# Two residual layers on two images: a convolution that splits each row once, keeps it in a ring and joins its sums, with the attention's instructions in another order

## The chip, the cores and the metric

The kernel runs on one core of a Trainium2 chip. The metric is the device time of one execution in microseconds. Five engines take part: PE multiplies matrices, DVE, ACT and POOL work on tensors, and SP issues all DMAs from one queue. Each runs its own list of instructions in order and waits on semaphores. PE writes only to PSUM (8 banks of 512 f32 per partition), and POOL doesn't read PSUM.

## The reference

The input x holds two images of 128 channels x 128 x 128 pixels. Two layers follow one another, each with a group normalisation `_gn` over 4 channels and all pixels of an image, and each added to its input:

```python
x = x + _L0_conv_ref(_gn(x), ...)   # windowed attention
x = x + _L1_conv_ref(_gn(x), ...)   # 3x3 convolution, 128 to 128 channels, bias
```

The attention works on g = clip((x * ac_w + ac_b) * x, 0, 6), takes q, k and v from it by a 384 x 128 matrix, does softmax(q k' / sqrt(8)) v in 16 heads of 8 channels within windows of 8 x 8 pixels, and multiplies by a 128 x 128 matrix.

## The kernel before

The channels are the partitions, and one image (`img`, 64 KB per partition) is resident. For each image the stages are: coefficients of the first normalisation, 32 units of attention, coefficients of the second normalisation, 16 strips of convolution. While image 0 is convolved, strips of image 1 are loaded into the rows that come free, and DVE takes their statistics (L784).

A unit of attention is 8 windows, 512 pixels. It passes through a software pipeline that spans about eight iterations; `iterations` calls `one(i, m, live)` on every engine, and the written order inside `one` is the order of that engine's list. The order isn't planned by any program: it is written out by hand, with iteration n working on unit n + lead. The steps of a unit are:

- DVE makes the affine part (L700), the product with x (L658) and the clip (L672). ACT casts it to half precision, `g_hi` (L503), and POOL takes the rest, `g_lo` (L369).
- PE projects q and k (`project`, L824 to L826, three half-precision products in place of a full-precision one) and v (`v_rows`, L842). ACT and DVE split q and k into two halves (L493 and L690, L478 and L688), and ACT copies v (L487).
- SP writes the halves of k and q to DRAM (L247, L248) and reads them back in another layout, `k_pl` (L266) and `q_bd` (L258).
- PE computes `scores` in four parts (L855), and DVE takes each part's row maxima (L646). Part p + 1 writes over part p in PSUM, so it waits for its maxima. PE transposes the maxima (L938), ACT and DVE split them (`m_pair`, L497 and L693), and SP copies them by four small DMAs as two further rows of `q_bd` (L274).
- PE computes the transposed scores with the maxima taken off (`scores_t`, L867), ACT exponentiates (L451), and PE multiplies with v and sums (`weigh`, L886, and L894 in parts 1 and 3). ACT and DVE divide (L458, L460, L639), POOL corrects the quotient by one Newton step (`quotient`, L361 and L363), PE projects it (L953), ACT scales (L470), POOL adds it to the image (L376), and DVE takes the statistics for the next normalisation (L684).

A strip of the convolution is 8 output rows. ACT normalises ten input rows into `cx` (L522). Each pair of neighbouring output columns comes from four planes of differences and sums of columns (64 columns each) instead of six products per row: DVE makes the planes 0 and 2 (L740), POOL the planes 1 and 3 (L399). ACT casts each to half precision (L528), and DVE takes the rest (`low`, L744). PE does 9 matmuls per plane, 36 of 512 columns per strip (L824 to L826), into one bank per plane; two sets of four banks alternate. ACT starts the odd columns from plane 1 with the bias (L512), DVE adds the planes by four instructions of 512 elements (`outputs_of`, L724), POOL adds the input (`residual`, L387), and SP stores the strip (L295). All ten rows of a strip are made anew, so two of ten are made twice.

What sets the order in a strip: DVE's list alternates L740 and L744 of strip t + 1 with the L724 of strip t - 1. POOL's L387 may start when all four L724 of its strip are done; `cx` may be overwritten when both DVE and POOL have made their planes.

## Time and profile before

| | us |
|---|---|
| median of 3 runs (1294.46 to 1301.38) | 1300.46 |
| profiled execution | 1303.66 |
| its span | 1301.9 |
| PE busy | 1058.8 (81%) |
| DVE busy | 1024.6 (79%) |
| ACT busy | 793.4 (61%) |
| POOL busy | 605.2 (46%) |
| mean granted clock of PE | 0.946 of 2.4 GHz |

The stages, read from the first and last instructions of their lines: the attention's residual L376 runs from 117.0 to 491.7 us and from 743.8 to 1118.1, the convolution's first normalisation starts at 498.97 in image 0, and the last instruction of the kernel ends at 1301.9. The time ahead of a stage's first L376 is the load, the coefficients and the filling of the pipeline.

An engine's busy time contains the time in which an instruction has started and stands still. A matmul's end is modelled: matmuls of 512 columns are 0.38 us long on the page and follow each other at 0.22.

### The profile page before, as it was taken

How to read it: one execution, taken by the hardware profiler on the slowest of the kernel's cores; microseconds unless marked ns; L12 is line 12 of the kernel's file. 1: busy time of each engine (PE TensorE's matmuls, PEld its weight loads, DVE VectorE, ACT ScalarE, POOL GpSimd, SP SyncE). 2: the span in 40 equal slices, each digit the busy share in tenths (PEclk: the TensorE clock that was granted, in tenths of full speed). 3: DMA queues.
4: the chain of work that ended last, by engine and by line, in shares of the span. 5: the costliest groups of instructions: out<-in, count | busy, mean ns of one | idle time of the engine just before them, and what ended most of it. 6: DMA issues, size and time to landing. Idle time of an engine off the chain costs nothing. (4 is left out here: it accounts for less than half of the span.)

```text
span 1301.9 us, 52825 instructions
## 1 busy us (share of the span) xinstructions
PE 1058.8 (81%) x23011; PEld 582.1 (45%) x23011; DVE 1024.6 (79%) x1315; ACT 793.4 (61%) x1295; POOL 605.2 (46%) x501
## 2 busy tenths in 40 slices
PE   1179999989998975887855999999999998498886
PEld 1045555555555542333322555555555555243332
DVE  6866787778887646999996677777787774599998
ACT  1147877777787764544412777777777776454442
POOL 7004444444444354555541344445445444366665
PEclk9999999999999996999885999999999999698998
DMA  7054444435444400222234544445444441001112
GB/s 284 25 147 122 134 130 132 140 113 145 123 133 127 138 19 1 97 98 97 97 114 139 138 130 137 127 128 140 133 132 129 138 141 30 1 33 48 49 50 80
DMA packets 114918, 140.60 MB, mean 108 GB/s; under 512 B 25088, under 2 KB 91008, under 8 KB 113664
## 3 DMA queue, kind: packets, MB, share of 16 engines
q1 hardware_dynamic: 114688, 137.23, 35.2%
q8 instruction: 182, 2.98, 1.0%
q14 instruction: 48, 0.39, 0.1%
HBM read 67.96 MB, written 67.11 MB: 104 GB/s over the span
## 5 line engine op out<-in xcount | busy, mean ns | idle before, releaser
L646 DVE TENSOR_REDUCE m_all<-ps 128x16 f32<-128x1024 f32 x256 | 312.8, 1222 | 134.2 <-PE ps L855 133.7
L369 POOL TENSOR_TENSOR g_lo<-work,g_hi 128x512 f16<-128x512 f32 x64 | 91.6, 1431 | 301.1 <-ACT g_hi L503 301.1
L361 POOL TENSOR_SCALAR work<-work 128x256 f32<-128x256 f32 x128 | 114.2, 892 | 210.2 <-DVE work L639 191.9
L824 PE MATMUL ps<-work,c_hi 128*128 128x512 f16 x384 | 153.5, 400 | 64.3 <-DVE work L744 64.3
L528 ACT CAST work<-work 128x640 f16<-128x640 f32 x128 | 91.9, 718 | 151.6 <-DVE work L740 118.0
L867 PE MATMUL ps<-q_bd,k_pl 128*64 128x256 f16 x2048 | 164.3, 283 | 18.2 <-DMA q_bd<-m_pair 13.0
L451 ACT ACTIVATE work<-ps,ws 128x1024 f32<-128x1024 f32 x128 | 142.7, 1115 | 40.8 <-PE ps L867 39.0
L855 PEld LDWEIGHTS ps<-k_pl,q_bd 48*64 48x64 f16 x8192 | 88.7, 111 | 155.1 <-issue 75.4
L744 DVE TENSOR_TENSOR work<-work 128x640 f16<-128x640 f32 x128 | 152.3, 1193 | 4.3 <-ACT work L528 4.2
L451 ACT ACTIVATE late_probs<-ps,ws 128x1024 f32<-128x1024 f32 x128 | 141.6, 1106 | 20.4 <-PE ps L867 20.4
L825 PE MATMUL ps<-work,c_lo 128*128 128x512 f16 x384 | 152.7, 398 | 0.0
L826 PE MATMUL ps<-work,c_hi 128*128 128x512 f16 x384 | 152.7, 398 | 0.0
L855 PE MATMUL ps<-k_pl,q_bd 48*64 48x64 f16 x8192 | 117.5, 198 | 39.5 <-DMA q_bd<-stack_scratch 27.5
L399 POOL TENSOR_TENSOR work<-work 128x640 f32<-128x640 f32 x64 | 113.5, 1774 | 51.0 <-DVE work L744 23.8
L387 POOL TENSOR_TENSOR work<-work,img 128x1024 f32<-128x1024 f32 x30 | 87.0, 2900 | 99.6 <-DVE work L724 99.6
L867 PEld LDWEIGHTS ps<-q_bd,k_pl 128*64 128x64 f16 x2048 | 93.5, 110 | 64.7 <-ACT late_probs L451 25.5
L639 DVE TENSOR_TENSOR work<-ps,work 128x512 f32<-128x512 f32 x128 | 87.3, 682 | 27.3 <-ACT work L460 27.3
L824 PEld LDWEIGHTS ps<-work,c_hi 128*128 128x128 f16 x384 | 38.8, 101 | 137.4 <-DVE work L744 96.4
L487 ACT COPY v_ext<-ps 64x256 f32<-64x256 f32 x256 | 93.1, 364 | 9.4 <-PE ps L842 4.8
L363 POOL TENSOR_TENSOR work<-work 128x256 f32<-128x256 f32 x128 | 93.2, 728 | 10.7
L740 DVE TENSOR_TENSOR work<-work 128x640 f32<-128x640 f32 x64 | 94.7, 1482 | 4.0 <-issue 2.4
L458 ACT ACTIVATE work<-ps 128x256 f32<-128x256 f32 x128 | 49.2, 384 | 74.8 <-PE ps L894 74.8
(128 smaller groups left out, 2008.7 us busy)
## 6 DMA issues: line engine op xcount, KB each, us to landing
stack_scratch<-work SPq DMA_DIRECT2D x128, 256.0 KB, 2.0
k_pl<-stack_scratch SPq DMA_DIRECT2D x128, 192.0 KB, 3.7
q_bd<-stack_scratch SPq DMA_DIRECT2D x256, 96.0 KB
stack_scratch<-work SPq DMA_DIRECT2D x128, 128.0 KB, 2.1
out_dram<-work SPq DMA_DIRECT2D x32, 512.0 KB, 2.6
img<-in_x_dram SPq DMA_DIRECT2D x8, 1024.0 KB, 13.5
img<-in_x_dram SPq DMA_DIRECT2D x16, 512.0 KB, 4.2
q_bd<-m_pair SPq DMA_DIRECT2D x256, 8.0 KB
```

The source lines that it names most:

```text
L361: g.tensor_scalar(near[h], near[h], -2.0, None, ALU.add).then_inc(less_done, 1)
L363: g.tensor_tensor(o_n[:, HALF * h:HALF * h + HALF], near[h], scaled[h], ALU.mult).then_inc(o_done, 1)
L399: g.tensor_tensor(plane[2 * k + 1], column(cx, 1), column(cx, c), op).then_inc(odd_planes, 1)
L451: a.activation(probs[h][:, p % 2, :], ps[:, ST_B:ST_B + 2, :].rearrange("p w t -> p (w t)"), ACT.Exp, scale=ws[:, R_EXP:R_EXP + 1]).then_i ...
L646: v.tensor_reduce(m_all[:, 0, :, p], ps[:, S_B:S_B + 2, :].rearrange("p r (a k) -> p (r a) k", k=WIN), AX.X, ALU.max).then_inc(max_done, 1)
L740: v.tensor_tensor(plane[2 * k], column(cx, a), column(cx, c), ALU.subtract).then_inc(even_planes, 1)
L744: v.tensor_tensor(x_lo[:, i, :, :], plane[i], x_hi[:, i, :, :], ALU.subtract).then_inc(x_lo_done, 1)
L824: t_.matmul(o, lhs_hi, rhs_hi, start=first, stop=False)
L825: t_.matmul(o, lhs_lo, rhs_hi, start=False, stop=False)
L826: return t_.matmul(o, lhs_hi, rhs_lo, start=False, stop=last)
L855: mm = t_.matmul(ps[64 * w:64 * w + 64, S_B + r, at:at + WIN], q_bd[rows, md, r, g, j, tok], k_pl[rows, md, g, tok], start=True, stop=True)
L867: mm = t_.matmul(ps[64 * c:64 * c + 64, ST_B + w, a * 256:a * 256 + 256], k_pl[:, md, g, tok], q_bd[:, md, :, g, :, tok], start=True, stop ...
```

## The change

In the convolution:

- Each input row is normalised, turned into planes and split only once, 8 new rows a strip (9 in the first). The halves go into a ring of 18 rows (`x_both`): strips with even t use the rows 0 to 9, those with odd t the rows 8 to 17. After every odd strip DVE copies the last two rows of all 8 half-planes to the front (`carry`, new L765).
- DVE makes all four planes (new L752); POOL makes none.
- ACT starts both column sets of the output from plane 1 (`bases`, new L512). DVE adds the planes 0 and 3 by one instruction over both sets (`ends`, new L727) and plane 2 by another that reads the bank twice (`middle_sums`, new L734). The odd set is kept negated, and POOL subtracts it.
- POOL adds the residual in two halves (new L397, L400); the half for even columns waits for the second plane of the strip three further on, that for odd columns for its fourth. There are three output buffers instead of two.
- `cx` lies where `g_hi` and `g_lo` lie during the attention.

In the attention, each engine's list has another order, and five iterations run ahead of the first unit and three behind the last (before: six and two). The arithmetic, the tiles and the number of buffers are as before. The diff, cut to its core:

```diff
-FIRST = 6
-LAST = 2
+FIRST = 5
+LAST = 3
...
-HALO = CROWS + 2
+XROWS = CROWS + 1
+RING = 2 * CROWS + 2
+OUTS = 3
...
-        cx = part(0, HALO * WIDE).rearrange("p (r c) -> p r c", r=HALO)
-        plane = [part(1300 + i * 640, 640).rearrange("p (r c) -> p r c", r=HALO) for i in range(PLANES)]
-        x_hi = part(3860, 1280).bitcast(F16).rearrange("p (i r c) -> p i r c", i=PLANES, r=HALO)
-        x_lo = part(5140, 1280).bitcast(F16).rearrange("p (i r c) -> p i r c", i=PLANES, r=HALO)
-        c_out = [part(6420 + i * 1024, 1024).rearrange("p (r c) -> p r c", r=CROWS) for i in range(2)]
+        cx = g_both[:, 0:XROWS * WIDE].rearrange("p (r c) -> p r c", r=XROWS)
+        plane = [part(i * XROWS * (SIDE // 2), XROWS * (SIDE // 2)).rearrange("p (r c) -> p r c", r=XROWS) for i in range(PLANES)]
+        x_both = part(2304, PLANES * RING * (SIDE // 2)).bitcast(F16).rearrange("p (k i r c) -> p k i r c", k=2, i=PLANES, r=RING)
+        x_hi, x_lo = x_both[:, 0, :, :, :], x_both[:, 1, :, :, :]
+        c_out = [part(6912 + i * 1024, 1024).rearrange("p (r c) -> p r c", r=CROWS) for i in range(OUTS)]
...
+        def carries(b, t):
+
+            return b * (CUNITS // 2 - 1) + (t - 1) // 2
+
+        def ring_rows(t):
+
+            at = CROWS * (t % 2)
+            return slice(at + (1 if t == 0 else 2), at + RING - CROWS)
+
+        def new_rows(t):
+
+            return slice(0 if t == 0 else 1, XROWS)
+
+        def column(t, s):
+
+            return cx[:, new_rows(t), s:s + SIDE - 1:2]
 
         def outputs(buf, s):
 
...
+        def halves(buf):
+
+            return buf.rearrange("p r (c e) -> p e (r c)", e=2)
+
...
                     if live(3):
+                        queries_in(n + 3, (m + 3) % BUFS)
                         keys_in(n + 3, (m + 3) % BUFS)
-                        queries_in(n + 3, (m + 3) % BUFS)
+                    if live(2):
+                        maxima(n + 2, (m + 2) % BUFS)
                     if live(4):
+                        after(sp, q_in, n + 1)
+                        write(0, n + 4, (m + 4) % BUFS, q_lo_done, q_sent)
                         after(sp, k_in, n + 1)
                         write(1, n + 4, (m + 4) % BUFS, k_lo_done, k_sent)
-                        after(sp, q_in, n + 1)
-                        write(0, n + 4, (m + 4) % BUFS, q_lo_done, q_sent)
-                    if live(2):
-                        maxima(n + 2, (m + 2) % BUFS)
                 iterations(b, one)
...
-                def residual(t, n, par, strip=None):
-                    after(pool, m3_out, n)
-                    after(pool, m2_out, n)
-                    x1 = img[:, bass.ds(t * CROWS, CROWS), :] if strip is None else strip[:, :, :]
-                    g.tensor_tensor(c_out[par][:, :, :], c_out[par][:, :, :], x1, ALU.add).then_inc(cadd_done, 1)
-
-                def conv_one(t, par, top, bottom):
+                def residual(t, n, spared):
+
+                    c = outputs_view(n)
+                    x1 = (kept[t - CUNITS + 2] if spared and t >= CUNITS - 2 else img[:, t * CROWS:t * CROWS + CROWS, :])
+                    x1 = x1.rearrange("p r (c e) -> p (r c) e", e=2)
+                    after(pool, sums_out, n)
+                    if t < CUNITS - 4:
+                        after(pool, planes_done, n + 3, 2)
+                    g.tensor_tensor(c[:, :, 0], c[:, :, 0], x1[:, :, 0], ALU.add).then_inc(cadd_done, 1)
+                    if t < CUNITS - 4:
+                        after(pool, planes_done, n + 3, 4)
+                    g.tensor_tensor(c[:, :, 1], x1[:, :, 1], c[:, :, 1], ALU.subtract).then_inc(cadd_done, 1)
+
...
+                def bases(n):
...
+                    after(act, out_done, n - OUTS)
...
+                    for e, (col, bias) in enumerate(((R_CONV, vecs[:, 3:4]), (R_MINUS, cf[:, C_MINUS:C_MINUS + 1]))):
+                        a.activation(outputs(c_out[n % OUTS], e), ps[:, PLANES * (n % 2) + 1, :], ACT.Identity,
+                                     scale=ws[:, col:col + 1], bias=bias).then_inc(base_out, 1)
...
+                    def high(i, t, n):
+                        after(act, planes_done, n, i + 1)
+                        if t % 2 == 0:
+                            after(act, conv_done, n - 1, i + 1)
+                        elif t > 1:
+                            after(act, carried, carries(b, t - 2))
+                        a.copy(x_hi[:, i, ring_rows(t), :], plane[i][:, new_rows(t), :]).then_inc(x_hi_done, 1)
...
+                    if not top:
+                        bases(n - 1)
                     if not bottom:
-                        normed(t + 1, n + 1, 0, HALO - before_last(t))
-                    high(3, n)
-                    if not bottom:
-                        high(0, n + 1)
-                        high(1, n + 1)
-                    if not bottom or b + 1 == BATCH:
-                        first_out(n, par)
-                    if not bottom:
-                        high(2, n + 1)
+                        for i in range(PLANES):
+                            high(i, t + 1, n + 1)
+                    if t + 2 < CUNITS:
+                        normed(t + 2, n + 2)
+                    if bottom and b + 1 == BATCH:
+                        bases(n)
...
+                    if live(1):
+                        after(dve, m_hi_done, n + 1)
+                        v.scalar_tensor_tensor(out=m_pair[:, 1, :], in0=ps[0:PAIRS * HEADS, M_B, 0:P], scalar=1.0 / PAIR_MAX,
+                                               in1=m_pair[:, 0, :], op0=ALU.mult, op1=ALU.subtract).then_inc(m_lo_done, 1)
+                    if live(3):
+                        after(dve, q_hi_done, n + 3)
+                        v.tensor_tensor(qk[:, 0, :], ps[:, GA, :], qk[:, 1, :], ALU.subtract).then_inc(q_lo_done, 1)
+                        after(dve, k_hi_done, n + 3)
+                        v.tensor_tensor(qk[:, 3, :], ps[:, GB, :], qk[:, 2, :], ALU.subtract).then_inc(k_lo_done, 1)
...
+                def ends(n):
+
+                    bank = PLANES * (n % 2)
+                    after(dve, base_out, n)
+                    after(dve, conv_done, n)
+                    c = halves(c_out[n % OUTS])
+                    v.scalar_tensor_tensor(out=c, in0=ps[:, bank:bank + PLANES:PLANES - 1, :], scalar=ws[:, R_CONV:R_CONV + 1], in1=c,
+                                           op0=ALU.mult, op1=ALU.add).then_inc(ends_out, 1)
+
+                def middle_sums(n):
+
+                    after(dve, ends_out, n)
+                    c = halves(c_out[n % OUTS])
+                    v.scalar_tensor_tensor(out=c, in0=ps[:, PLANES * (n % 2) + 2, :].unsqueeze(1).broadcast_to([P, 2, 512]),
+                                           scalar=ws[:, R_CONV:R_CONV + 1], in1=c, op0=ALU.mult, op1=ALU.add).then_inc(sums_out, 1)
...
+                        v.tensor_tensor(x_lo[:, i, ring_rows(t), :], plane[i][:, new_rows(t), :], x_hi[:, i, ring_rows(t), :],
+                                        ALU.subtract).then_inc(x_lo_done, 1)
+
+                    def carry(n):
+
+                        after(dve, conv_done, n - 1)
+                        after(dve, x_lo_done, n)
+                        flat = x_both.rearrange("p k i r c -> p (k i) (r c)")
+                        w = SIDE // 2
+                        v.tensor_copy(flat[:, :, 0:2 * w], flat[:, :, (RING - 2) * w:RING * w]).then_inc(carried, 1)
...
+                        plane_of(1, t + 1, n + 1)
+                    if not top:
+                        ends(n - 1)
+                    if t % 2 and not bottom:
+                        carry(n)
+                    if not bottom:
+                        low(0, t + 1, n + 1)
+                        plane_of(2, t + 1, n + 1)
+                        low(1, t + 1, n + 1)
+                        plane_of(3, t + 1, n + 1)
+                    if not top:
+                        middle_sums(n - 1)
+                    if not bottom:
+                        low(2, t + 1, n + 1)
+                        low(3, t + 1, n + 1)
...
+                        after(pe, sums_out, b * CUNITS - 1)
+                    if live(-1):
+                        weigh(n - 1, (m - 1) % BUFS, 3)
                     if live(0):
                         after(pe, m_in, n)
                         scores_t(n, m, 0)
+                    if live(1):
+                        scores(n + 1, (m + 1) % BUFS, 2)
                     if live(2):
                         if live(2):
                             after(pe, q_lo_done, n + 2)
                         else:
                             after(pe, v_out, n + 1)
                         v_rows((m + 2) % BUFS)
+                    if live(3):
+                        if live(-2):
+                            after(pe, res_done, n - 2)
+                        else:
+                            after(pe, k_lo_done, n + 2)
+                        after(pe, g_lo_done, n + 3)
...
-                    if live(2):
-                        after(pe, q_in, n + 2)
-                        after(pe, k_in, n + 2)
-                        scores(n + 2, (m + 2) % BUFS, 0)
...
+                    if live(2):
+                        after(pe, q_in, n + 2)
+                        after(pe, k_in, n + 2)
+                        scores(n + 2, (m + 2) % BUFS, 0)
+                    if live(0):
                         scores_t(n, m, 3)
```

PE in the attention, from behind the projection of q to that of the result (L855 scores, L938 transpose of the maxima, L867 scores_t, L886 and L894 weigh, L953 projection of the result), before:

```order
L855 MATMUL ps<-k_pl,q_bd 64x64 x32
L938 MATMUL ps<-ident,m_all 128x128
L867 MATMUL ps<-q_bd,k_pl 64x256 x8
L886 MATMUL ps<-work,v_ext 32x64 x16
L894 MATMUL ps<-work,adds 32x256 x8
L867 MATMUL ps<-q_bd,k_pl 64x256 x8
L886 MATMUL ps<-late_probs,v_ext 32x64 x16
L953 MATMUL ps<-work,pw 128x512
```

and now (L876 scores, L964 transpose, L888 scores_t, L907 and L915 weigh, L984 projection):

```order
L964 MATMUL ps<-ident,m_all 128x128
L888 MATMUL ps<-q_bd,k_pl 64x256 x8
L907 MATMUL ps<-work,v_ext 32x64 x16
L915 MATMUL ps<-work,adds 32x256 x8
L876 MATMUL ps<-k_pl,q_bd 64x64 x32
L888 MATMUL ps<-q_bd,k_pl 64x256 x8
L907 MATMUL ps<-late_probs,v_ext 32x64 x16
L984 MATMUL ps<-work,pw 128x512
```

The first part of scores (L855 at the head, now L876) moved from ahead of the transpose to behind the first weighing with sums.

PE from the second part of scores on, with the last weighing of the unit (L886, L894), the projection of k (L824 to L826), scores 2 and scores_t 0, before:

```order
L855 MATMUL ps<-k_pl,q_bd 64x64 x32
L886 MATMUL ps<-late_probs,v_ext 32x64 x16
L894 MATMUL ps<-late_probs,adds 32x256 x8
L824 MATMUL ps<-g_hi,w_hi 128x512
L825 MATMUL ps<-g_hi,w_lo 128x512
L826 MATMUL ps<-g_lo,w_hi 128x512
L855 MATMUL ps<-k_pl,q_bd 64x64 x32
L867 MATMUL ps<-q_bd,k_pl 64x256 x8
```

and now (L876 scores 1, L907 and L915 the last weighing, L888 scores_t 0, L876 scores 2, L863 the first matmuls for v):

```order
L876 MATMUL ps<-k_pl,q_bd 64x64 x32
L907 MATMUL ps<-late_probs,v_ext 32x64 x16
L915 MATMUL ps<-late_probs,adds 32x256 x8
L888 MATMUL ps<-q_bd,k_pl 64x256 x8
L876 MATMUL ps<-k_pl,q_bd 64x64 x32
L863 MATMUL ps<-w_hi,g_both 128x128 x2
L863 MATMUL ps<-w_lo,g_both 128x128
```

The projection of k and scores 2 stood between the last weighing and scores_t 0. Scores_t 0 now follows the weighing at once, and the projection of k stands behind v.

DVE in one strip of the convolution (L740 planes, L744 low parts, L724 sums), before:

```order
L740 TENSOR_TENSOR work<-work 128x640
L744 TENSOR_TENSOR work<-work 128x640
L740 TENSOR_TENSOR work<-work 128x640
L724 SCALAR_TENSOR_TENSOR work<-ps,ws,work 128x512
L744 TENSOR_TENSOR work<-work 128x640
L724 SCALAR_TENSOR_TENSOR work<-ps,ws,work 128x512 x2
L744 TENSOR_TENSOR work<-work 128x640
L724 SCALAR_TENSOR_TENSOR work<-ps,ws,work 128x512
L744 TENSOR_TENSOR work<-work 128x640
```

and now (L752 planes, L756 low parts, L727 and L734 joined sums, L765 carry):

```order
L752 TENSOR_TENSOR work<-g_both 128x512 x2
L727 SCALAR_TENSOR_TENSOR work<-ps,ws,work 128x2x512
L765 COPY work<-work 128x8x128
L756 TENSOR_TENSOR work<-work 128x512
L752 TENSOR_TENSOR work<-g_both 128x512
L756 TENSOR_TENSOR work<-work 128x512
L752 TENSOR_TENSOR work<-g_both 128x512
L734 SCALAR_TENSOR_TENSOR work<-ps,ws,work 128x2x512
L756 TENSOR_TENSOR work<-work 128x512 x2
```

Four planes and four low parts of 512 elements stand in place of two and four of 640, and two sums of 1024 elements in place of four of 512.

In SP's list the maxima (L274, now L286) were issued behind the writes of k and q and ahead of the next reads. They now stand behind the reads and ahead of the writes, and q goes ahead of k.

## Rows read from the trace of the kernel before

**Rows 1.** Windows in attention and convolution: us, busy us by engine (x instructions), PEclk, DMA share, GB/s.

```profile
900.00:1000.00 100.00, 93.59 (x2734) 56.48 (x2728) 78.32 (x104) 77.73 (x137) 47.23 (x49) 1.00 0.48 131
...
1200.00:1250.00 50.00, 39.12 (x174) 15.72 (x172) 50.00 (x47) 22.10 (x28) 30.43 (x15) 1.00 0.14 54
```

**Rows 2.** Timeline of DVE, convolution of image 1: start us, us, engine, line, operation.

```profile
1202.11 2.97 DVE L740 TENSOR_TENSOR work<-work 128x640 f32<-128x640 f32 x1
...
1206.81 0.81 DVE L740 TENSOR_TENSOR work<-work 128x640 f32<-128x640 f32 x1
1207.54 0.75 DVE L724 SCALAR_TENSOR_TENSOR work<-ps,ws,work 128x512 f32<-128x512 f32 x1
...
1212.80 2.97 DVE L740 TENSOR_TENSOR work<-work 128x640 f32<-128x640 f32 x1
```

**Rows 3.** Timeline of POOL, same stretch.

```profile
1201.53 2.86 POOL L387 TENSOR_TENSOR work<-work,img 128x1024 f32<-128x1024 f32 x1 [3.47 <-DVE work L724]
...
1207.03 1.72 POOL L399 TENSOR_TENSOR work<-work 128x640 f32<-128x640 f32 x1 [0.83 <-DVE work L744]
```

**Rows 4.** Timeline of DVE, convolution of image 0: the statistics of two strips.

```profile
567.04 1.27 DVE L784 BATCH_NORM_STATS2 st<-img 128x6 f32<-128x512 f32 x2
...
577.73 1.27 DVE L784 BATCH_NORM_STATS2 st<-img 128x6 f32<-128x512 f32 x2
```

**Rows 5.** Timeline of POOL: the attention's residual of units 0, 28 of each image.

```profile
116.97 1.27 POOL L376 TENSOR_TENSOR img<-img,work 128x512 f32<-128x512 f32 x1
...
468.69 1.28 POOL L376 TENSOR_TENSOR img<-img,work 128x512 f32<-128x512 f32 x1
...
743.82 1.27 POOL L376 TENSOR_TENSOR img<-img,work 128x512 f32<-128x512 f32 x1
...
1093.14 1.27 POOL L376 TENSOR_TENSOR img<-img,work 128x512 f32<-128x512 f32 x1
```

**Rows 6.** Waits of PE from 117 to 1093 us: total us, times, longest us.

```profile
PE ps L855 <- DMA q_bd<-stack_scratch: 26.7, 33, 1.6
...
PE ps L824 <- ACT v_ext L487: 12.3, 53, 1.1
PE ps L867 <- DMA q_bd<-m_pair: 10.4, 16, 1.7
```

**Rows 7.** Groups by line and shape, whole span: busy us, mean ns | idle before.

```profile
L646 DVE TENSOR_REDUCE m_all<-ps 128x16 f32<-128x1024 f32 x256 | 312.8, 1222 | 134.2 <-PE ps L855 133.7
...
L744 DVE TENSOR_TENSOR work<-work 128x640 f16<-128x640 f32 x128 | 152.3, 1193 | 4.3 <-ACT work L528 4.2
...
L740 DVE TENSOR_TENSOR work<-work 128x640 f32<-128x640 f32 x64 | 94.7, 1482 | 4.0 <-issue 2.4 <-ACT work L522 1.5
...
L672 DVE TENSOR_SCALAR work<-work 128x512 f32<-128x512 f32 x64 | 26.8, 418 | 2.4 <-POOL g_lo L369 2.2
```

**Rows 8.** Timeline of PE: first and last of 13 matmuls in a row.

```profile
1266.06 0.38 PE L826 MATMUL ps<-work,c_hi 128*128 128x512 f16 x1
...
1268.65 0.38 PE L826 MATMUL ps<-work,c_hi 128*128 128x512 f16 x1
```

**Rows 9.** Timeline of all engines: from the transpose of the maxima to their DMAs.

```profile
257.62 0.33 PE L938 MATMUL ps<-ident,m_all 128*128 128x128 f32 x1
...
258.70 0.27 DVE L693 SCALAR_TENSOR_TENSOR m_pair<-ps,m_pair 64x128 f16<-64x128 f32 x1
...
258.91 1.05 PE L894 MATMUL ps<-work,adds 128*32 128x256 f32 x16
...
259.75 4.08 SPq L274 DMA_DIRECT2D q_bd<-m_pair  x4
```

**Rows 10.** Timelines of SP's queue and PE: maxima, keys, and who waited.

```profile
337.40 3.51 SPq L274 DMA_DIRECT2D q_bd<-m_pair  x4
...
341.01 1.97 SPq L266 DMA_DIRECT2D k_pl<-stack_scratch  x2
...
343.83 0.63 PE L867 MATMUL ps<-q_bd,k_pl 128*64 128x256 f16 x8 [1.09 <-DMA q_bd<-m_pair]
```

More of the change, by code:

```diff
@@ L317, in _ @@
+                    if more and t < CUNITS - 2:
+                        after(sp, cx_done, n + 1)
+                        after(sp, next_in, t - 1)
+                        refill(t, next_in)
                 conv_units(conv_one)
@@ L371, in one @@
                         quotient(n - 1, 0)
[L372 to L378 removed]
                 def last_unit():
[L380 removed]
+                    residual(CUNITS - 1, b * CUNITS - 1, True)
@@ L774, in conv_one @@
+                    if more and t > 2:
+                        strip_stats(t - 3)
+                    if more and bottom:
+                        for k in range(CUNITS - 3, CUNITS):
+                            strip_stats(k)
                     if bottom and not more:
-                        outputs_of(n, par)
+                        sums(n)
                 def strip_stats(s):
```

299 lines of the change are left out of this document (110 added, 189 removed).

## The prediction

> **What bounds the kernel now.** I read the windows by stage first, to see which engine is full where. In the attention stage PE is busy 93.59 of 100 us at full clock; in the convolution stage DVE is busy 50.00 of 50.00 and PE 39.12 [rows 1]. The two stages have different owners, so each part of the change is priced in its own stage.
>
> For the convolution I read the timeline of DVE against that of POOL, because a full engine need not be one that works. One strip of eight output rows takes 10.69 us (L740 at 1202.11, the next at 1212.80) [rows 2]. The same L740 takes 0.81 us at 1206.81 and 2.97 at 1202.11; there POOL's residual (L387) had begun at 1201.53 and ended at 1204.39, and DVE ended 0.69 after it [rows 2, 3]. So a DVE operation with both inputs in SBUF stands still until POOL's is over. L724, which reads one input from PSUM, takes 0.75 at 1207.54 with POOL's L399 beside it. The strip of image 0 contains two statistics instructions more (1.27 us) and is still 10.69 us long (567.04 to 577.73) [rows 4]: the work that image 1 lacks is made up by standing still. From one start to the next an operation costs 0.08 less than its duration (0.73 for 0.81 at 1206.81), so L724 costs 0.66. Free of POOL, a strip of image 1 on DVE is 6 x 0.73 + 4 x 0.66 = 7.0 us. 3.7 of its 10.69 us are POOL's doing, partly through waits for POOL's planes; that is what can be won.
>
> For the attention I read the waits of PE. A unit (512 pixels) takes 12.56 us in image 0 (116.97 to 468.69, 28 units) and 12.48 in image 1 (743.82 to 1093.14, 28 units) [rows 5]. From the first of these marks to the last, PE waits for the queries' read 26.7 us, for v's copies on ACT 12.3 and for the maxima's copy 10.4 [rows 6]: 49.4 us, of which some are the ramp of image 1's; at most 0.88 for each of the 56 units. PE's own list is thus 12.52 - 0.88 = 11.64 us long, or a little more: 11.7.
>
> **The convolution, part by part.** DVE gets the two planes that POOL made, and all eight operations on planes shrink from 640 to 512 elements, since two halo rows are kept. By proportion one costs 0.73 x 0.8 = 0.58 at least, and 0.65 if only the 0.81 of duration shrinks in proportion; I take 0.61. Eight: 4.9. The four L724 (4 x 0.66 = 2.64) become two over 1024 elements. The trace has a 1024-element reduction from PSUM at 1.22 [rows 7] as the lower end and 2 x 0.66 = 1.32 as the upper; I take 1.2 from start to start, 2.4 for both. The carry, seven per image of 1024 half-precision elements, isn't in the trace: L672 moves the same bytes in 0.42 [rows 7], and 1.2 is the cost at one element a step; I take 0.6, or 0.3 per strip. Nothing is gained or lost elsewhere by it: low 0 of the next strip queues behind it.
>
> POOL keeps only the residual, in halves of about 1.3 us (2.86 for the whole, part of it standing). Each half waits until DVE has made two planes and is about to read PSUM for 1.2 us, so it covers all but some 0.2 us of each half: 0.4 per strip. Sum for image 1: 4.9 + 2.4 + 0.3 + 0.4 = 8.0 us; image 0 has the statistics too: 9.2.
>
> The Trainium skill (SBUF — State Buffer, section "Who interferes with whom") says that a copy in a two-port mode, like a two-input operation, contends with GpSimd, and that the one that starts second waits for the whole of the other. By it the carry stands behind the first residual half wherever that outlasts the sums; at 0.2 us seven times an image it changes the sum by under 3 us. That lock is what L740 shows [rows 2, 3].
>
> What comes next is PE: 12 spacings take 2.59 us, so 36 matmuls take 7.77 us at full clock [rows 8]. Image 1 at 8.0 sits just above that floor. PE has a whole strip of slack: the sums of strip t-1 stand in DVE's round t, and low 0 of t+1 right behind them. ACT gets one base more and smaller casts; it is busy 22.10 of 50 us [rows 1], no bound. The casts of even strips wait for the previous strip's matmuls plane by plane, the last for all 7.8 us of them; its low part is wanted three quarters of a strip later still, so that stays off the path.
>
> Savings: 14 x (10.69 - 9.2) = 21 us in image 0, 14 x (10.69 - 8.0) = 38 in image 1. The ends: the last strip has 2.4 instead of 2.9 us of sums and the same residual and store. I take 1 us. The first strip fills as before (its DVE list is longer, POOL's share in series before).
>
> **The attention.** No arithmetic changes. The first scores of unit n+2 move from ahead of the transpose of the maxima (257.62) to behind the second weighing of unit n, whose last matmuls (L894) end at 258.91 + 1.05 = 259.96: 2.3 us later [rows 9]. The longest wait for the queries was 1.6. The projection of k moves between v and that of q, 0.65 us (three matmuls of the conv's spacing) over a usual wait of 0.2. Both should vanish, 39 of the 49 us. Against this stands the maxima's path. In the list before, the transpose (257.62) led to L693 (258.70) and, past four writes in SP's queue, to the maxima's DMAs at 259.75: 2.13 us [rows 9]. Now they stand ahead of the writes and L693's successor stands ahead of the low parts: some 1.1 us. But the first transposed scores now follow the last weighing at once, so they come 1.2 us earlier. The gain and the loss about cancel; SP still waits before them for the reads of the next unit (L266, two in 1.97 [rows 10]).
>
> New tight places: scores 2, row maximum, scores 3 now leave some 1.9 us (v and k's projection between) for a maximum that takes 1.22 with 0.5 ahead of it. I add 0.2 us to PE's 11.7: 11.9. Bounds: 11.5, a little under PE's list, since some waits may hide behind the modelled ends of matmuls; 12.6, nothing won. Savings: 56 x (12.52 - 11.9) = 35 us. Ramps: one iteration fewer ahead and one more behind, the same dependent chain; nothing taken, plus or minus 3 us.
>
> **Sum** against the profiled execution, 1303.66 us: 1303.7 - 21 - 38 - 1 - 35 = 1209. The median of the runs was 3 us lower than that execution, so I say 1206.
>
> **The rivals.** A: the maxima become the attention's loop. The four DMAs took 3.51 us to issue and landed 2.92 us later (337.40, PE went on at 343.83) [rows 10]; from transposed scores 0 to the next transpose the new list has 4.8 us of PE work. 1.1 + 6.4 + 4.8 = 12.3 us per unit: the attention saves 12 us instead of 35, and the time is 1229. For it: PE waited for them 16 times already. Against it: they queued behind four fresh writes, now behind reads that are some 2 us old. The Trainium skill (DMA: Bandwidth & Descriptors, section "Queues, rings and completion order") says that an engine consumes a ring's descriptors in order, so the maxima now stand behind the keys' reads. That is this rival's mechanism.
>
> B: DVE's durations don't fall, because POOL's halves collide as its planes did. L744 and L740 average 1.19 and 1.48 us over the kernel [rows 7]; at 0.8 of that, a strip is 4 x 0.95 + 4 x 1.18 + 2.7 = 11.2 us, and 12.4 with statistics: plus 24 and plus 7. With the attention's 35 that is 1297, no change to speak of. Against it: POOL was busy 30.43 of 50 us [rows 1], 6.5 per strip; the new list has 2.6.
>
> C, slower: the writes now stand behind the maxima. If SP's round (3.5 for the maxima, then the four writes, their landing, the queries' and the keys' reads, of which the keys' are 1.97 [rows 10] and the rest an estimate of 5 together: 10.5 in all) takes its slow values, 4.1 for the maxima [rows 9] and another microsecond in the reads, the keys land after PE wants them and every unit waits. It decides from 12.52 + 60/56 = 13.6 us per unit; at 13.8 the time is 1304 - 60 + 72 = 1316.
>
> D: PE's list has slack that the rows don't show, a unit takes 11.5 and a strip of image 1 is bound by PE at 7.8: 1303 - 21 - 41 - 57 = 1184, 1181 as a median.
>
> **Chances.** Forecast 0.60, A 0.17, D 0.12, B 0.05, C 0.04, other 0.02. The forecast's own range is 1190 to 1222; with A and D inside, and leaving B and C out, 1176 to 1245. About 0.5% (6.5 us) is what this kernel's runs can tell from no change. Forecast, A and D are faster: with part of B 0.92; same 0.04; slower 0.04.
>
> **What would show it.** Two-input operations on 512 elements at about 0.68 us with few at twice that; the joined sums at 1.3; strips of 9.2 and 8.0 us; no wait of scores for the queries' read; units of 11.9 with PE's clock at 1.00. The prediction is wrong if a strip is not under 10 us, if PE's waits for the maxima exceed 0.5 us a unit, or if DVE has a new wait for ACT's normalisation.

## The result and the profile after

The changed kernel takes 1219.97 us (median of four runs, 1213.3 to 1225.59); the kernel before took 1300.92 beside it (four runs). The ratio is 0.937, 95% interval 0.930 to 0.945: 81 us faster. The prediction said 1206. The profiled execution of the changed kernel is its fastest, 1213.3 us, with a span of 1211.6; what is read from its attention is thus some 7 us too good in sum, and the separation of the parts below goes by the medians of runs. (The convolution doesn't vary: that of image 0 takes 161.0 us here, and 161.0 and 160.9 in e10 and e5, which leave it as it is.)

The aggregation of the statistics ends each stage, so three of its starts cut the span into attention and convolution of either image (the first piece has the load and the first statistics too). Timeline of DVE, those rows alone:

```profile
475.61 1.02 DVE L610 BATCH_NORM_AGGREGATE sc<-st 128x2 f32<-128x192 f32 x1
...
636.58 1.02 DVE L610 BATCH_NORM_AGGREGATE sc<-st 128x2 f32<-128x192 f32 x1
...
1059.99 1.02 DVE L610 BATCH_NORM_AGGREGATE sc<-st 128x2 f32<-128x192 f32 x1
```

In the kernel before, the same marks stood at 493.7, 672.69 and 1120.13. So the stages went from 493.7, 179.0, 447.4 and 181.8 us to 475.6, 161.0, 423.4 and 151.6: 18.1, 18.0, 24.0 and 30.2 us saved, 42 in the attention and 48 in the convolution, 90 together.

Windows of the attention of either image and of the convolution of either image (columns as in [rows 1]):

```profile
250.00:350.00 100.00, 94.02 (x2814) 58.61 (x2806) 86.22 (x109) 79.53 (x140) 48.93 (x50) 1.00 0.46 137
810.00:910.00 100.00, 97.23 (x2974) 61.52 (x2976) 90.24 (x113) 83.86 (x150) 52.05 (x52) 1.00 0.48 144
520.00:600.00 80.00, 70.91 (x322) 30.02 (x320) 80.00 (x108) 43.88 (x62) 26.03 (x18) 1.00 0.36 119
1100.00:1180.00 80.00, 79.43 (x366) 34.67 (x364) 80.00 (x105) 49.34 (x70) 29.53 (x20) 1.00 0.16 65
```

The convolution of image 1 now has both engines full: DVE 80.00 and PE 79.43 of 80. In image 0 DVE alone is full. In the attention PE still idles for 3 to 6 us of 100.

Timeline of DVE in the convolution of image 1, one strip (what was [rows 2]):

```profile
1139.83 1.27 DVE L727 SCALAR_TENSOR_TENSOR work<-ps,ws,work 128x1024 f32<-128x1024 f32 x1
1141.02 1.09 DVE L756 TENSOR_TENSOR work<-work 128x512 f16<-128x512 f32 x1
1142.04 0.68 DVE L752 TENSOR_TENSOR work<-g_both 128x512 f32<-128x512 f32 x1
...
1143.85 1.27 DVE L734 SCALAR_TENSOR_TENSOR work<-ps,ws,work 128x1024 f32<-128x1024 f32 x1
1145.04 1.62 DVE L756 TENSOR_TENSOR work<-work 128x512 f16<-128x512 f32 x2
```

And POOL beside it (what was [rows 3]):

```profile
1140.05 1.51 POOL L397 TENSOR_TENSOR work<-work,img 128x512 f32<-128x512 f32 x1 [2.50 <-DVE work L752]
1144.00 1.51 POOL L400 TENSOR_TENSOR work<-img,work 128x512 f32<-128x512 f32 x1 [2.43 <-DVE work L752]
```

L727 and L734 are the joined sums, L752 the planes, L756 the low parts. POOL's half starts at 1140.05 and ends at 1141.56, the sum L727 gives over to L756 at 1141.02, and L756 lasts 1.09 instead of 0.68: it stood still for 0.41 us. The same happens at 1145.04, where two L756 take 1.62 instead of 1.28. From one L727 to the next it is 8.30 and 7.96 us in turn, the longer with the carry. Image 0 alternates between 9.48 and 9.14.

Timeline of POOL: the attention's residual of units 0 and 28 of each image (what was [rows 5]):

```profile
116.43 1.27 POOL L382 TENSOR_TENSOR img<-img,work 128x512 f32<-128x512 f32 x1
...
450.44 1.28 POOL L382 TENSOR_TENSOR img<-img,work 128x512 f32<-128x512 f32 x1
...
709.85 1.27 POOL L382 TENSOR_TENSOR img<-img,work 128x512 f32<-128x512 f32 x1
...
1036.33 1.28 POOL L382 TENSOR_TENSOR img<-img,work 128x512 f32<-128x512 f32 x1
```

28 units in 334.01 and in 326.48 us are 11.93 and 11.66 us each. Waits of PE from 116 to 450 us (total, times, longest; before: [rows 6], over both images):

```profile
PE ps L876 <- issue: 15.5, 20, 2.0
PE ps L876 <- DVE m_all L650: 1.9, 2, 1.3
...
PE ps L888 <- DMA q_bd<-m_pair: 0.4, 2, 0.2
```

The waits for v's copies are gone and those for the maxima nearly so. L876 is the scores, and "issue" names no releaser. What it waits for had to be found.

Timeline of PE around a unit without a wait and one with it (L907 is a weighing, the fourth of a unit at 900.52 and 911.65; L964 the transpose of the maxima; L863 the first matmuls for v, L845 the projection of k behind them; L876 at 920.47 scores 0):

```profile
900.52 0.66 PE L907 MATMUL ps<-late_probs,v_ext 128*32 128x64 f32 x32
...
902.90 0.29 PE L863 MATMUL ps<-w_hi,g_both 128*128 128x128 f16 x2
...
903.58 0.38 PE L845 MATMUL ps<-g_both,w_hi 128*128 128x512 f16 x1
...
906.50 0.27 PE L964 MATMUL ps<-ident,m_all 128*128 128x128 f32 x1
...
911.65 0.65 PE L907 MATMUL ps<-late_probs,v_ext 128*32 128x64 f32 x32
...
920.47 0.45 PE L876 MATMUL ps<-k_pl,q_bd 48*64 48x64 f16 x32 [0.56 <-issue]
```

Timeline of SP's queue between:

```profile
907.48 2.43 SPq L286 DMA_DIRECT2D q_bd<-m_pair  x4
910.31 0.99 SPq L259 DMA_DIRECT2D stack_scratch<-work  x1
...
913.42 2.77 SPq L270 DMA_DIRECT2D q_bd<-stack_scratch  x4
916.29 0.79 SPq L278 DMA_DIRECT2D k_pl<-stack_scratch  x2
918.61 3.50 SPq L286 DMA_DIRECT2D q_bd<-m_pair  x4
```

The unit without a wait, 900.52 to 911.65, is 11.13 us: that is PE's own list. The wait is at scores 0 of unit n+2 (920.47), as are 17 of the 20 from 116 to 450 us (14.6 of 15.5 us stand right behind L915). The queue shows the way there: the maxima at 907.48, the writes, the queries at 913.42, the keys at 916.29 to 917.08, and 3.4 us later PE goes on. From that came a theory, which I call SP's round: SP issues the maxima once the transpose is through, then four writes, waits for them, then six reads, and the reads' landing releases scores 0 of the next iteration. The rival was the prediction's: a unit of 11.7 is PE's own list.

### The profile page after: what moved, and what is told of

It is laid out like the page before. It is cut to its first block, busy times and chain, and to the rows that moved or that the text cites. A ratio compares the mean times of both kernels' runs of the same rounds, so it can differ in the third digit from the quotient of the medians.

```text
span 1211.6 us, 52709 instructions
## 1 busy us (share of the span) xinstructions
PE 1013.6 (84%) x23011; PEld 581.7 (48%) x23011; DVE 996.8 (82%) x1331; ACT 791.0 (65%) x1327; POOL 503.9 (42%) x469
## 4 chain that ended last, share of the span: by engine, by line
PE 64%; DVE 19%; issue 8%; DMA 3%; ACT 2%; SPq 2%; POOL 2%; POOLq 0%; DVEq 0%; ACTq 0%
PE ps L907 12%; PE ps L888 11%; PE ps L915 9%; PE ps L876 8%; PE ps L984 5%; PE ps L845 5%; DVE work L756 5%; PE ps L846 5%; PE ps L847 5%; DVE work L752 4%; PE ps L863 4%; DVE st L602 1%; DVE work L734 1%; DVE st L805 1%; SPq L286 1%
## 5 line engine op out<-in xcount | busy, mean ns | idle before, releaser
L367 POOL TENSOR_SCALAR work<-work 128x256 f32<-128x256 f32 x128 | 108.6, 848 | 389.4 <-DVE work L643 370.6
L845 PE MATMUL ps<-work,c_hi 128*128 128x512 f16 x384 | 148.5, 387 | 31.6 <-DVE work L756 31.6
L876 PEld LDWEIGHTS ps<-k_pl,q_bd 48*64 48x64 f16 x8192 | 90.0, 111 | 165.0 <-issue 121.0
L888 PE MATMUL ps<-q_bd,k_pl 128*64 128x256 f16 x2048 | 162.8, 281 | 6.8 <-ACT work L450 4.0
L876 PE MATMUL ps<-k_pl,q_bd 48*64 48x64 f16 x8192 | 118.6, 198 | 50.6 <-issue 34.6
L532 ACT CAST work<-work 128x512 f16<-128x512 f32 (+1 forms) x128 | 78.9, 622 | 117.7 <-DVE work L752 106.4
L847 PE MATMUL ps<-work,c_hi 128*128 128x512 f16 x384 | 147.9, 385 | 0.0
L846 PE MATMUL ps<-work,c_lo 128*128 128x512 f16 x384 | 147.8, 385 | 0.0
L377 POOL TENSOR_TENSOR g_both<-work,g_both 128x512 f16<-128x512 f32 x64 | 100.2, 1565 | 78.0 <-ACT g_both L468 78.0
L888 PEld LDWEIGHTS ps<-q_bd,k_pl 128*64 128x64 f16 x2048 | 92.8, 110 | 57.5 <-issue 23.1
L397 POOL TENSOR_TENSOR work<-work,img 128x512 f32<-128x512 f32 x30 | 48.1, 1602 | 143.9 <-DVE work L752 129.2
L756 DVE TENSOR_TENSOR work<-work 128x512 f16<-128x512 f32 (+1 forms) x128 | 100.6, 805 | 5.1 <-ACT work L532 4.8
L752 DVE TENSOR_TENSOR work<-g_both 128x512 f32<-128x512 f32 (+1 forms) x128 | 85.8, 692 | 4.0 <-issue 2.1
L907 PE MATMUL ps<-late_probs,v_ext 128*32 128x64 f32 x4096 | 86.5, 222 | 1.9 <-issue 1.9
L907 PE MATMUL ps<-work,v_ext 128*32 128x64 f32 x4096 | 84.3, 223 | 0.0
## 6 DMA issues: line engine op xcount, KB each, us to landing
img<-in_x_dram SPq DMA_DIRECT2D x8, 1024.0 KB, 11.9
```

The lines of the kernel that those rows point to most:

```text
L367: g.tensor_scalar(near[h], near[h], -2.0, None, ALU.add).then_inc(less_done, 1)
L752: v.tensor_tensor(plane[i][:, new_rows(t), :], column(t, l), column(t, r), op).then_inc(planes_done, 1)
L756: v.tensor_tensor(x_lo[:, i, ring_rows(t), :], plane[i][:, new_rows(t), :], x_hi[:, i, ring_rows(t), :], ALU.subtract).then_inc(x_lo_done, 1)
L845: t_.matmul(o, lhs_hi, rhs_hi, start=first, stop=False)
L846: t_.matmul(o, lhs_lo, rhs_hi, start=False, stop=False)
L847: return t_.matmul(o, lhs_hi, rhs_lo, start=False, stop=last)
```

## The experiments

### The two parts alone

```
e1: before.py; the `one` lists of the attention on all engines as in the new kernel, FIRST = 5, LAST = 3
e2: the new kernel; the `one` lists as before, FIRST = 6, LAST = 2
```

> The kernel before with the new lists of the attention alone; its convolution is the old one. Theory (the two parts add): the attention's share is 35 us by the prediction, and 42 by the stages of the new kernel's trace, so 1259 to 1266 us. Rival (part of the attention's gain comes from the new convolution, which leaves the next attention a better start or other addresses): 1275 us or more.

Measured: 1267.7 us (1261.95 to 1274.79), ratio 0.977 [0.971, 0.982], against 1299.87 for the kernel before: 32 us. Units of 11.97 and 11.84 us.

> The new kernel with the old lists of the attention on all five engines; only the convolution is new. Theory: strips of 9.3 and 8.1 us and an attention unit of 12.5: 48 us saved by the stages of the new kernel's trace, 60 by the prediction, so 1241 to 1253 us; with the attention's part it adds up to the 81 us of the whole change. Rival (the convolution's gain is smaller alone, the attention's larger): over 1260 us.

Measured: 1252.86 us (1251.07 to 1254.61), ratio 0.964 [0.962, 0.967]: 47 us. Strips of 9.33 and 8.34 us on average over 12, units of 12.58 and 12.50.

32 and 47 are together 79 of the 81 us. The parts add; neither needs the other. The attention alone came out 1.7 us outside the range of the theory, since the 42 us of the profiled execution are those of the fastest run.

### What POOL's residual still costs

```
e3, POOL:
-                    if t < CUNITS - 4:
-                        after(pool, planes_done, n + 3, 2)
-                    if t < CUNITS - 4:
-                        after(pool, planes_done, n + 3, 4)
e4, POOL:
-  g.tensor_tensor(c[:, :, 0], c[:, :, 0], x1[:, :, 0], ALU.add)
+  g.tensor_tensor(c[:, 0:1, 0], c[:, 0:1, 0], x1[:, 0:1, 0], ALU.add)
   (and so for the other half)
```

> The new kernel with each residual half shrunk to one element per partition: the residual is left out, its waits and signals stay. Theory (what is left of POOL's lock is 0.8 us per strip): image 0 saves 15 x 0.8 = 12 us, image 1 falls to PE's 7.77 us per strip and saves 15 x 0.36 = 5 us, so 1203 us, and the strips are 8.5 and 7.8 us. Rival (the long L756 are DVE's own): no change, 1220 us.

Measured: 1201.43 us (1195.05 to 1208.43), 18.5 less than the new kernel. Strips of 8.49 and 7.77 us on average over 12 (9.33 and 8.33 in the new kernel, counted the same way), L756 at 686 ns instead of 805. So 0.8 us per strip is what is left of POOL in image 0, as the theory had it. In image 1 PE now ends the strip: 7.77 is its floor of [rows 8], and the window from 1090 to 1170 us shows it busy throughout:

```profile
1090.00:1170.00 80.00, 80.00 (x372) 36.32 (x371) 77.16 (x109) 50.00 (x73) 4.00 (x21) 1.00 0.17 68
```

The rival falls.

> The new kernel, but the residual's halves on POOL don't wait for planes of the strip after next; they start when the joined sums are done. Theory (DVE stands still behind POOL wherever it wants two operands of SBUF): the halves now meet low 2 and low 3 instead of the sums; each blocks 1.0 us more than now, 2 us per strip in 24 strips: some 1220 + 45 = 1265 us, with L756 near 1.5 on average. Rival (the place of a half is indifferent, since two engines only share bandwidth): within 6 us of the new kernel, 1214 to 1226 us.

Measured: 1239.81 us (1235.39 to 1246.17), ratio 0.955 [0.950, 0.959]: 20 us more than the new kernel, and not the 45 expected. The place does matter; the size expected was wrong. The low parts average 795 ns, not 1500, and it is the planes that got longer (914 ns instead of 692). The timelines of DVE and POOL in one strip of image 0 show why. Lines are four lower in this run: L752 are the low parts, L748 the planes, L801 the statistics, L395 and L396 the residual's halves.

```profile
555.90 1.28 DVE L752 TENSOR_TENSOR work<-work 128x512 f16<-128x512 f32 x2
557.11 1.27 DVE L801 BATCH_NORM_STATS2 st<-img 128x6 f32<-128x512 f32 x2
558.30 2.70 DVE L748 TENSOR_TENSOR work<-g_both 128x512 f32<-128x512 f32 x2
```

```profile
556.06 2.48 POOL L395 TENSOR_TENSOR work<-work,img 128x512 f32<-128x512 f32 x1 [5.43 <-DVE work L730]
558.51 1.94 POOL L396 TENSOR_TENSOR work<-img,work 128x512 f32<-128x512 f32 x1
```

Here POOL came second: its half lasts 2.48 instead of 1.51 us because DVE's pair L752 had begun at 555.90, and it then ran beside the statistics, which keep their 1.27. Only the second half met a pair of planes (2.70 instead of 1.28). The stop works in both directions, and the statistics, which read one operand from SBUF, are free of it. The half-precision copy L765 reads one operand too and isn't: behind POOL's half it takes 0.82 us instead of 0.42. The Trainium skill (SBUF — State Buffer, section "Who interferes with whom") says that whichever of the two starts first blocks the other for its whole instruction, and that a DVE instruction with at most one SBUF input is free of it outside the two-port modes, which a copy can enter. The trace agrees: 1.27 for the statistics with POOL beside them, 2.48 for POOL behind DVE.

### SP's round or PE's list

```
e5, SP:     for r in range(HR):
-               for k in range(2):
+               for k in range(1):          # and m_in counts 32
e6, SP:     maxima(n + 2) moved behind write(0, ...) and write(1, ...)
e7, PE:     scores(n + 2, ..., 0) with its waits moved ahead of the transpose
e8, PE:     scores(n + 2, ..., 0) with its waits moved behind scores_t(n, m, 3)
```

> The new kernel with two of the four DMAs of the maxima left out (those of their low halves, so the scores are shifted by a rounded maximum). Theory (what is left of PE's waits in the attention is SP's round: maxima 2.4 to 3.5 us, writes, landing, queries, keys, and scores 0 waits for the keys; PE's own list is 11.13 us, the distance of two units without a wait): the round is 1.2 to 1.7 us shorter, the waits marked issue at the scores go, the unit falls to 11.2, and the time by 56 x 0.6 = 34 us to 1186. Rival (a unit of 11.7 is PE's own list, as the prediction had it): within 6 us of the new kernel, 1214 to 1226 us.

Measured: 1184.08 us (1182.7 to 1185.91), ratio 0.909 [0.905, 0.913]; 36 us less than the new kernel. Units of 11.38 and 11.31 us, half of them under 11.15. In the stretch from 116 to 450 us PE's waits at the scores fell from 15.5 to 3.1:

```profile
PE ps L876 <- issue: 3.1, 7, 1.0
```

> The new kernel with SP's maxima back behind the four writes; PE, ACT and DVE keep the new lists. Theory (the maxima's path decides here: by the trace they land just in time, and 2.5 us of writes would stand ahead): PE waits for them at the transposed scores 0, the unit is 13 to 14, 1290 to 1340 us. Rival (SP's place of the maxima is indifferent, since the reads gain what they lose): within 10 us of the new kernel.

Measured: 1340.2 us (1336.29 to 1344.03). Units of 13.68 and 13.91 us. PE's waits over the span:

```profile
PE ps L888 <- DMA q_bd<-m_pair: 125.9, 60, 3.8
```

60 waits, nearly one per unit, for the maxima's landing at the transposed scores 0. With the new lists of the other engines and the maxima at their old place in SP's, the kernel is slower than the one before (1302.81 beside it): the new order is one piece over the engines.

> The new kernel with the first scores of unit n+2 back ahead of the transpose on PE, 2.2 us earlier in the list. Theory (SP's round ends at these scores, and it is as long as the list now leaves it): every us of earlier place is a us of unit, 13.5 to 14 us, up to 1335. Rival (the prediction's view, a wait of 0.5 us per unit comes back): 1250 us.

Measured: 1366.64 us (1362.12 to 1369.4), 32 over what the theory gave at most. Units of 14.29 and 14.24 us. PE's waits over the span:

```profile
PE ps L876 <- issue: 114.9, 50, 4.6
```

This is also what ties "issue" at L876 to the reads: with these scores 2.2 us earlier in the list the same wait grows from 34.6 us (40 times) over the span to 114.9, and six more waits of L876 are named in this run, four for the queries' read (10.1 us) and two for the keys' (3.0). A part of the excess may be PE's clock; the window from 200 to 400 us:

```profile
200.00:400.00 200.00, 173.89 (x4888) 106.27 (x4886) 144.78 (x186) 137.66 (x243) 83.63 (x85) 0.93 0.39 118
```

PE was idle for 26 of 200 us and was granted 0.93 of its clock, where the new kernel has 1.00. How much of the miss that is no run shows; the rest is open.

> The new kernel with the first scores of unit n+2 one place later, behind the transposed scores 3, 0.56 us. Theory (SP's round ends at them): the unit falls by 0.3 to 0.5 us towards PE's list of 11.13, 1195 to 1205 us. Rival (the row maximum on DVE between scores 0 and scores 1 then becomes short of room): no gain or a loss, 1220 us or more.

Measured: 1219.01 us (1216.51 to 1222.24): no gain. PE's waits over the span:

```profile
PE ps L876 <- issue: 23.4, 20, 4.4
PE ps L876 <- DVE m_all L650: 21.1, 40, 2.9
```

The waits for the reads fell from 34.6 to 23.4, those for the row maxima rose from 15.4 to 21.1. The rival came true in its effect, not in its place: the marked waits for row maxima stand at scores 3 (0.16 to 0.17 us, 14 of them from 116 to 450 us), not between scores 0 and 1. The maxima follow one another on DVE, and the shortest units are now 11.42 us instead of 11.13, which takes back what the reads gained. Moving the scores isn't the way; the round has to become shorter.

### The kernel before under the same knife

```
e12: before.py with the change of e5
```

> The kernel before (old lists, old convolution) with the DMAs of the low halves of the maxima left out. Theory (in the kernel before too the unit was SP's round, and PE's own list was not 11.7 but some 11.2 us): the unit falls from 12.5 to about 11.5, the time to 1300 - 56 = 1245 us. Rival (PE's list of 11.7 as the prediction had it, only part of the waits goes): the unit stays over 11.8, 1260 us or more.

Measured: 1263.57 us (1260.31 to 1266.02), ratio 0.972 [0.969, 0.976]; 36 us less than before. Units of 11.92 and 11.92 us. The theory's 11.5 and 1245 failed, and the rival's bounds, over 11.8 and 1260 or more, are met. The round cost 0.6 us per unit there too, but what is left is not 11.2. Timeline of PE, a unit of this run:

```profile
904.30 1.05 PE L894 MATMUL ps<-late_probs,adds 128*32 128x256 f32 x16
905.28 0.39 PE L824 MATMUL ps<-g_hi,w_hi 128*128 128x512 f16 x1
...
906.97 0.23 PE L842 MATMUL ps<-w_hi,g_hi 128*128 128x128 f16 x1
...
907.59 0.22 PE L842 MATMUL ps<-w_lo,g_hi 128*128 128x128 f16 x1
907.82 0.45 PE L855 MATMUL ps<-k_pl,q_bd 48*64 48x64 f16 x32
...
908.80 0.65 PE L886 MATMUL ps<-work,v_ext 128*32 128x64 f32 x32
909.67 0.39 PE L824 MATMUL ps<-g_hi,w_hi 128*128 128x512 f16 x1 [0.21 <-ACT v_ext L487]
...
916.10 1.05 PE L894 MATMUL ps<-late_probs,adds 128*32 128x256 f32 x16
```

From 904.30 to 916.10 it is 11.80 us with one marked wait of 0.21: the old list is 11.6 us of its own, the new one 11.13. The same matmuls, 0.46 us apart, both at a granted clock of 1.00. The two timelines show where. The twelve matmuls for v take 0.85 us from the first to what follows, the scores (906.97 to 907.82), and 0.68 in the new list, where k's projection follows (902.90 to 903.58). The projection of q takes 0.75 with scores behind it (909.67 to 910.42) and 0.66 with the transpose (905.84 to 906.50). L886 to L824 is 0.87 here, of which 0.21 is the marked wait, and 0.59 in the new kernel. The scores behind v (0.43 and 0.38) and the transpose (0.25 and 0.20) give 0.05 each. That is 0.43 of the 0.46: what a group of matmuls costs depends on what stands behind it. Why it does is open.

### A faster version

```
e9, DVE, image 0:
                    if not top:
                        ends(n - 1)
+                   if more and t > 3:
+                       half_stats(t - 4, 1)
...
                        middle_sums(n - 1)
+                   if more and t > 2:
+                       half_stats(t - 3, 0)
-                   if more and t > 2:
-                       strip_stats(t - 3)
e10:
-   m_pair = sb("m_pair", [PAIRS * HEADS, 2, P], F16)
+   m_pair = sb("m_pair", [P, P], F16)             # rows 64r: high, 64r + 32: low
SP, for r in range(HR):
-       for k in range(2): at = 64 * r + ROWS + k
-           sp.dma_start(q_bd[at:at + 1, ...], m_pair[32 * r:32 * r + 32, k, :])
+       at = 64 * r + ROWS
+       sp.dma_start(q_bd[at:at + 2, ...], m_pair[64 * r:64 * r + 64, :])
DVE: m_lo in two instructions, from rows 64r to rows 64r + 32
```

> The new kernel, but image 0's two statistics instructions of a strip stand one behind each joined sum, in front of the low parts, instead of both at the round's end. Theory (a residual half of 1.51 us outlasts the sum of 1.27 by 0.3 to 0.4 us, and the next operation with two SBUF operands pays that; a one-input instruction of 0.6 us can stand there free): the L756 of 1.1 and 1.6 us fall to 0.68, a strip of image 0 is 8.5 to 8.6 instead of 9.3, 12 to 14 strips save 9 to 10 us: 1210 us. Rival (the statistics are blocked by POOL too, or the refills aren't there half a round earlier): no gain, 1220 us.

Measured: 1217.03 us (1215.02 to 1218.67, five runs), which the new kernel's own spread doesn't let one tell from 1220. The trace does: the convolution of image 0 takes 154.1 instead of 161.0 us, its strips alternate between 8.72 and 8.39. Groups of DVE from 500 to 600 us, first of the new kernel, then of this one:

```profile
L756 DVE TENSOR_TENSOR work<-work 128x512 f16<-128x512 f32 x43 | 33.8, 803 | 1.4 <-ACT work L532 1.4
L765 DVE COPY work<-work 128x1024 f16<-128x1024 f16 x5 | 4.1, 818 | 0.0
```

```profile
L756 DVE TENSOR_TENSOR work<-work 128x512 f16<-128x512 f32 x46 | 30.8, 684 | 2.4 <-ACT work L532 2.4
L765 DVE COPY work<-work 128x1024 f16<-128x1024 f16 x6 | 2.8, 472 | 0.0
```

The standing still is gone, also for the carry L765, at no instruction more. The stage gives 6.9 of the 9 to 10 us expected; the last strips of the image got longer (11.50 and 9.41 between L727s instead of 11.05 and 7.19).

> The new kernel with two DMAs for the maxima instead of four, of the same bytes: high and low maxima lie in neighbouring blocks of partitions, so one DMA carries both; DVE makes the low ones in two instructions of 32 partitions instead of one of 64 (about 0.25 us more). Theory (the attention's unit is SP's round, and SP pays per DMA): most of the 36 us of the run with half the maxima is had, 1187 to 1200 us, unit 11.3 to 11.5. Rival (SP pays per row moved, and there are as many rows as before): 1220 us or a little more.

Measured: 1188.11 us (1184.03 to 1188.89), ratio 0.914 [0.911, 0.917]; units of 11.32 and 11.36 us. SP's queue:

```profile
907.57 1.10 SPq L285 DMA_DIRECT2D q_bd<-m_pair  x2
...
914.65 0.93 SPq L278 DMA_DIRECT2D k_pl<-stack_scratch  x2
```

The same rows and bytes in two DMAs take 1.10 us of SP where four took 2.43 to 3.50. So it is the number of DMAs that SP pays for here, not the bytes. That gives 32 us, nearly the 36 of the run that left half of the maxima's data out. (The maxima's DMAs are L285 in this run.)

> The statistics split and the merged maxima together. They touch different stages, so the gains add: 1220 - 10 - 25 = 1185 us, range 1177 to 1197. If one of them fails, the sum falls short by just that one's share.

Measured: 1178.78 us (1177.18 to 1181.53, six runs), ratio 0.907 [0.904, 0.909]: 41 us under the changed kernel, whose interval is 0.930 to 0.945, and 121 under the one before. The statistics give 9 us on top of e10, which could be told here because the runs lie closer together.

## Why the prediction was right, and where it was not

The total was right, 1206 against 1220 and inside the range, though not every term. The parts, each alone, saved 47 us in the convolution where 60 were forecast (e2), and 32 in the attention where 35 were (e1). That the attention's sum came so near is partly luck, as its two terms below show. Of the signs named, the steady strips under 10 us, the waits for the maxima (0.4 us from 116 to 450 us) and the clock of 1.00 were met; that the scores wait for no read was not.

- **Two-input operations of 512 elements at 0.61 from start to start, 0.68 long.** Measured 0.60 and 0.68.
- **Joined sums at 1.2.** 1.20 from start to start.
- **0.2 us left over of each residual half.** It was 0.4. The halves last 1.51 us, not the 1.3 taken from half of the whole residual, and stand behind a sum of 1.2. With the carry delayed as well (0.81 where it takes 0.42 alone) a strip came to 8.13 and 9.31 instead of 8.0 and 9.2. e4 shows that this is POOL, since it goes with the halves' length while their waits and signals stay, and that without it PE's 7.77 ends the strip.
- **PE has slack in the convolution, its floor is 7.77.** Right as a floor. With PE at 79.43 of 80 us, "a whole strip of slack" was true at a strip's scale but not over the image: at the end DVE waits 3.08 us for PE's last matmuls (L727 at 1202.89).
- **Savings of the convolution, 59 us plus 1.** 48 by the stages and 47 by e2. In image 0 it was 18.0 of 21 (14 strips of 9.31 would save 19). The step that failed in image 1, 30.2 of 38, is the multiplication by 14 steady strips: there the time from the first joined sum (1080.29) to that of the last strip (1202.89) is 122.6 us in 15 intervals. Ten of them are steady and save 10 x 2.56 = 26 us. The other five take 41.3 us, where the old kernel's five took some 42 (148.9 from the first L724 at 1144.59 to those of the last strip at about 1293.5, less ten of 10.69): they save 0.7 instead of the 11 counted. After the last planes the halves have nothing to wait for, run back to back and meet low parts and planes (L756 2.94 us at 1185.86, L752 2.33 at 1188.97, that strip 10.9 us long; in e4, with halves of one element, it takes 8.29); and in the first rounds DVE waits for ACT's casts and for PE. Against that the first sum came 4.2 us sooner after the statistics (20.3 instead of 24.5 us), where "fills as before" had been said. 26 + 1 + 4 are 31, the stage shows 30.2.
- **Queries' read and v's copies no longer waited for.** v's wait went, as said. The step that failed is the wait at scores 0: it was 26.7 us from 117 to 1093 us and is 30.8 from 116 to 1036, under another name. The position gained 2.3 us. That SP's new order took it back, because it puts the maxima ahead of the writes, is read from the queue; no run shows it apart, since in e6, with the maxima behind the writes, another wait sets the unit. The prediction weighed that order only for the maxima's own path.
- **PE's own list 11.7, plus 0.2 for tight places, 11.9 a unit.** The unit was right (11.93 and 11.66; 11.97 and 11.84 in e1), the two addends were not. The list is 11.13, the old one 11.6 (e12): subtracting the marked waits from the unit was good for the old list, and that the new order is itself shorter by 0.46 wasn't foreseen. What took its place is a wait of some 0.6 for SP's round (e5, e10). Two errors of about the same size cancelled, and that was luck.
- **Rival A, the maxima as the loop.** Its place was right and its form wrong. The maxima bind through SP's time to issue them, not by landing late; e6 shows what their landing late costs, 120 us.
- **Rival B, durations that don't fall,** is out: 0.68. **Rival C, keys late,** is the kernel's real bound in small: the keys' reads end SP's round. It makes the kernel slower, and by more than the 13.8 us per unit and 1316 us of this rival, only when scores 0 also stand at their old place: e7, 14.3 us per unit, 1367 us.
- **Rival D** is what the kernel comes to when both leftovers are cut: units of 11.3 in e10 and e11 (11.5 was said), 7.77 in e4.

## What to carry to other kernels

When an order is changed on several engines, follow the queue that issues DMAs as a list of its own: here the number of DMAs that SP issues, not their bytes, held the unit up, and two of the smallest DMAs fewer per unit were worth 32 us, as much as the whole reordering of the attention (e1). An operation that must run on POOL beside a full DVE starts together with instructions of DVE that it doesn't stop. Here these were the sums, which read one operand from SBUF and one from PSUM, and the statistics, but not the half-precision copy. They must last as long as POOL's operation; if they are too short, put another of that kind next to them (e9). The waits that a view names give a list's length for the order that was measured, not for another one: the same matmuls took 11.6 us in one order and 11.13 in the other.

## What was not expected of the hardware

- A small DMA (8 KB) costs SP 0.6 to 0.9 us to issue when four follow one another (2.43 to 3.50) and 0.55 in a pair of the same total bytes (1.10).
- DVE and POOL stop one another in both directions: 2.48 and 3.71 us for a POOL operation that takes 1.51 beside the joined sums (3.71 in e3 at 1136.80). A half-precision copy with a single input is stopped too (0.82 us instead of 0.42).
- The same matmuls differ by 0.46 us in 11.6 by their order alone, most of it where small matmuls for v or a projection are followed by scores.
